# Transformer block stage on one core: splitting the normalized rows on token partitions and turning the fp16 halves with transposing DMA transfers

## What is computed

```python
h = _L0_tok_ref(x)                                   # attention over the 512 positions -> (64, 32, 512)
h = h + _L0_attn_ref(_layernorm(h, axis=-1), Wq, Wk, Wv, Wo, qn_w, kn_w)
h = h + _L0_ffn_ref(_layernorm(h, axis=-1), w1, w2, w3)
# _L0_attn_ref: 16 query heads and 4 key heads of 128; RMS norm and rotary embedding of q and k; causal; @ Wo.T
# _L0_ffn_ref:  sigmoid(x @ q(w1).T) * (x @ q(w2).T) @ q(w3).T with ternary q(w), hidden width 1408
```

## Time and profile before

| | |
|---|---|
| median of 3 executions | 1176.59 us (1174.29 to 1178.07) |
| the profiled execution | 1181.81 us |
| its span, first to last instruction | 1179.9 us |
| granted TensorE clock, mean over the span | 0.964 |
| busy: PE / DVE / ACT / POOL | 1097.3 / 722.2 / 422.4 / 433.5 us |

### The profile page before, as it was taken

The page is one execution under the profiler, slowest core; times in us unless marked ns, Lnnn a source line. Parts: engine busy times, 40 slices in busy tenths (PEclk is TensorE's granted clock), DMA queues, the critical chain, the costliest instruction groups (busy, mean ns, idle before and its releaser), DMA issues.

```text
span 1179.9 us, 22172 instructions
## 1 busy us (share of the span) xinstructions
PE 1097.3 (93%) x8768; PEld 609.3 (52%) x8768; DVE 722.2 (61%) x1293; ACT 422.4 (36%) x733; POOL 433.5 (37%) x334
## 2 busy tenths in 40 slices
PE   4999998889989569999999999999999999999987
PEld 2434333343334234664665756646646657566465
DVE  6687766766686255556655755665566557656642
ACT  1666545545555221322322412323223223223231
POOL 2001016664555254242351451433423614524320
PEclk9999898989998779999999999999999999999999
DMA  6988833554442100000000000000000000000000
GB/s 181 315 298 260 299 115 115 158 176 124 140 130 69 57 9 10 20 9 27 18 9 27 0 27 18 9 27 18 9 27 18 9 27 0 27 18 9 18 11 9
DMA packets 35767, 83.81 MB, mean 71 GB/s; under 512 B 4496, under 2 KB 5264, under 8 KB 35728
## 3 DMA queue, kind: packets, MB, share of 16 engines
q1 hardware_dynamic: 35728, 83.26, 22.8%
HBM read 49.43 MB, written 8.39 MB: 49 GB/s over the span
## 4 chain that ended last, share of the span: by engine, by line
PE 51%; DVE 8%; issue 4%; POOL 2%; ACT 0%; DMA 0%; SPq 0%; DVEq 0%; POOLq 0%
PE proj L973 7%; PE proj L974 7%; PE proj L975 7%; PE ffn_sum L1025 5%; PE ffn_sum L1026 5%; PE proj L1087 4%; PE proj L1088 4%; PE proj L1089 4%; PE transposed L967 3%; PE ffn_sum L1073 2%; PE transposed L1041 1%; PE proj L1059 1%; PE proj L1060 1%; DVE probs_t L930 1%; DVE scores L910 1%
## 5 line engine op out<-in xcount | busy, mean ns | idle before, releaser
L334 DVE TENSOR_REDUCE row_max<-score_rows 128x1 f32<-128x512 f32 x256 | 167.7, 686 | 94.0 <-PE score_rows L474 92.6
L700 POOL TENSOR_TENSOR roped<-rope_cos,rope_sin 128x512 f32<-128x512 f32 x80 | 101.7, 1271 | 328.3 <-DVE rope_sin L836 328.3
L293 ACT ACTIVATE exps<-score_cols 128x512 f32<-128x512 f32 x256 | 146.2, 600 | 140.4 <-PE score_cols L499 137.9
L1025 PE MATMUL ffn_sum<-x_hi,ffn_w 128*128 128x128 f16 x1408 | 167.0, 220 | 1.4 <-ACT x_hi L769 1.4
L1026 PE MATMUL ffn_sum<-x_lo,ffn_w 128*128 128x128 f16 x1408 | 166.8, 220 | 0.0
L735 ACT ACTIVATE squares<-proj 128x512 f32<-128x512 f32 x80 | 47.8, 597 | 323.4 <-PE proj L975 289.5
L973 PE MATMUL proj<-attn_slots,x_hi 128*128 128x512 f16 x384 | 147.8, 385 | 3.7 <-DVE rope_sin L836 2.2
L974 PE MATMUL proj<-attn_slots,x_hi 128*128 128x512 f16 x384 | 147.7, 385 | 0.0
L975 PE MATMUL proj<-attn_slots,x_lo 128*128 128x512 f16 x384 | 147.5, 384 | 0.0
L474 PE MATMUL score_rows<-k_parts,q_parts 96*128 96x512 f32 x256 | 127.4, 511 | 16.5 <-DMA k_parts<-qk_low 15.2
L1025 PEld LDWEIGHTS ffn_sum<-x_hi,ffn_w 128*128 128x128 f16 x1408 | 138.1, 98 | 6.4 <-DVE hidden L853 3.0
(11 more groups left out here) (108 smaller groups left out, 1724.7 us busy)
## 6 DMA issues: line engine op xcount, KB each, us to landing
raw_ffn<-in_w_ffn SPq DMA_DIRECT2D x24, 704.0 KB, 7.2
attn_slots<-in_w_attn SPq DMA_DIRECT2D x20, 512.0 KB, 10.8
qk_raw<-in_qk SPq DMA_DIRECT2D x16, 512.0 KB, 5.8
q_parts<-qk_high SPq DMA_DIRECT2D x32, 256.0 KB, 3.3
k_parts<-qk_high SPq DMA_DIRECT2D x32, 256.0 KB, 4.2
v_t<-in_v_t SPq DMA_DIRECT2D x16, 256.0 KB, 5.7
q_parts<-qk_low SPq DMA_DIRECT2D x16, 256.0 KB, 4.9
k_parts<-qk_low SPq DMA_DIRECT2D x16, 256.0 KB, 5.2
```

The lines of the kernel that those rows point to most:

```text
L293: nc.scalar.activation(E[:, (STEPS * g + u) % NE, :], ST[(STEPS * g + u) % 3][:, :], ACT.Exp, scale=TOK_SCALE).then_inc(exp_done, 1)
L334: nc.vector.reduce_max(row_max[:, g % 2, k:k + 1], S[n % NS][:, :], AX.X).then_inc(s_free, 1)
L1025: nc.tensor.matmul(dst, w, x2h[:, k * P:(k + 1) * P], start=(k == 0), stop=False)
```

## The change

Both places where normalized rows are turned are changed alike. The split into halves now happens on the rows as they lie, before they are turned: ScalarE rounds `xn` (or `x2n`) into `x_hi_rows` (or its twin), the low half is `xn` minus that. Then SyncE issues, for each half, one DMA transfer with `transpose=True` (128x512 fp16, SBUF to SBUF, 128 KB) into `x_hi` / `x_lo`, now laid out [P, KD, P]. TensorE's eight fp32 transposes per tile for `xn` and `x2n` are gone, and it waits for the two transfers instead. Along with it:

- the low half of the first norm moves from VectorE to GpSimd (`x_low`, behind `inv_std` and ahead of `rope_sum(n+1, 0)`); that of the second norm stays on VectorE and moves ahead by one chunk, between `rotate(n, 2)` and `rotate(n, 3)`;
- on ScalarE the rounding of `x2n` moves from behind `square(n, 3)` to behind `square(n, 1)`, the rounding of `xn` from behind `hidden_hi(n-1, 2)` to right behind the Exp;
- SyncE's loop over tiles is written out tile by tile; there `turn_x2(n-1)` and `turn_x(n+1)` stand between the loads of the rows and the store of the output.

```diff
-        xh, xl = sb("x_hi", [P, D], F16), sb("x_lo", [P, D], F16)
+        xhr, xlr = sb("x_hi_rows", [P, D], F16), sb("x_lo_rows", [P, D], F16)
+        xh, xl = sb("x_hi", [P, KD, P], F16), sb("x_lo", [P, KD, P], F16)
...
@@ block.sync
+            def turn_x(n):
+                sp.wait_ge(x_hi, n + 1)
+                sp.dma_start(xh[:, :, :], xhr[:, :], transpose=True).then_inc(x_turned, DMA)
+                sp.wait_ge(x_lo, n + 1)
+                sp.dma_start(xl[:, :, :], xlr[:, :], transpose=True).then_inc(x_turned, DMA)
...
                 if attn:
                     sp.wait_ge(h2_done, n)
                     sp.dma_start(h_res[:, :], h1[bass.ds(n * P, P), :]).then_inc(res_in, DMA)
                 if ffn:
+                    turn_x2(n - 1)
+                if more:
+                    turn_x(n + 1)
+                if ffn:
                     sp.wait_ge(o_out, n + START)
                     sp.dma_start(out[bass.ds((n - 1) * P, P), :], o_tile[:, :]).then_inc(out_done, DMA)
...
-            over_tiles(sp, body)
+            for n in range(NTT + 1):
+                body(n, n < NTT, n > 0)
@@ block.gpsimd
+            def x_low(n):
+                pool.wait_ge(x_hi, n + 1)
+                nc.gpsimd.tensor_tensor(xlr[:, :], xn[:, :], xhr[:, :], ALU.subtract).then_inc(x_lo, 1)
@@ block.scalar
             def take_x(n):
-                act.wait_ge(xt, n + 1)
-                nc.scalar.copy(xh[:, :], TR[0][:, :]).then_inc(x_hi, 1)
+                act.wait_ge(ln1, n + 1)
+                nc.scalar.copy(xhr[:, :], xn[:, :]).then_inc(x_hi, 1)
...
                 if attn:
-                    for c in range(1, KV):
+                    square(n, 1)
+                if ffn:
+                    act.wait_ge(ln2, n)
+                    nc.scalar.copy(x2hr[:, :], x2n[:, :]).then_inc(x2_hi, 1)
+                if attn:
+                    for c in range(2, KV + 1):
                         square(n, c)
-                if ffn:
-                    act.wait_ge(xt2, n)
-                    nc.scalar.copy(x2h[:, :], TR[1][:, :]).then_inc(x2_hi, 1)
-                if attn:
-                    square(n, KV)
@@ block.vector
-            def x_low(n):
-                dve.wait_ge(x_hi, n + 1)
-                nc.vector.tensor_tensor(xl[:, :], TR[0][:, :], xh[:, :], ALU.subtract).then_inc(x_lo, 1)
...
                 if attn:
-                    for c in range(2, KV):
+                    rotate(n, 2)
+                if ffn:
+                    dve.wait_ge(x2_hi, n)
+                    nc.vector.tensor_tensor(x2lr[:, :], x2n[:, :], x2hr[:, :], ALU.subtract).then_inc(x2_lo, 1)
+                if attn:
+                    for c in range(3, KV + 1):
                         rotate(n, c)
@@ block.tensor
                 if c == 0:
-                    pe.wait_ge(x_hi, n + 1)
-                    pe.wait_ge(x_lo, n + 1)
+                    pe.wait_ge(x_turned, 2 * DMA * (n + 1))
...
                 if f == 0 and m == 0:
-                    pe.wait_ge(x2_hi, n + 1)
-                    pe.wait_ge(x2_lo, n + 1)
+                    pe.wait_ge(x2_turned, 2 * DMA * (n + 1))
```

More of the change, by code:

```diff
@@ L676, in _, with turn_x2 @@
                 sp.dma_start(dst, src).then_inc(const_in, DMA)
+            def turn_x(n):
[3 more added lines that the diff above has]
+                sp.dma_start(xl[:, :, :], xlr[:, :], transpose=True).then_inc(x_turned, DMA)
+            def turn_x2(n):
+                sp.wait_ge(x2_hi, n + 1)
+                sp.dma_start(x2h[:, :, :], x2hr[:, :], transpose=True).then_inc(x2_turned, DMA)
+                sp.wait_ge(x2_lo, n + 1)
+                sp.dma_start(x2l[:, :, :], x2lr[:, :], transpose=True).then_inc(x2_turned, DMA)
+            turn_x(0)
             def body(n, attn, ffn):
-                if attn and not (isinstance(n, int) and n + 1 >= NTT):
+                more = attn and not (isinstance(n, int) and n + 1 >= NTT)
+                if more:
                     sp.wait_ge(ln1, n + 1)
@@ L783, in body @@
                             nc.scalar.activation(pr[:, :, :], sd[:, :, :], ACT.Exp).then_inc(exped, 1)
+                            if not last:
+                                take_x(n + 1)
                         if ffn and m == 1:
@@ L786, in body @@
                 if attn:
-                    if not last:
-                        take_x(n + 1)
                     act.wait_ge(pv, n + 1)
@@ L934, in body @@
                 if attn:
-                    if not last:
-                        x_low(n + 1)
                     for b in range(2):
@@ L1024, in gate_products @@
                         dst = FB[2 * (f % 2) + m][:, j * P:(j + 1) * P]
-                        nc.tensor.matmul(dst, w, x2h[:, k * P:(k + 1) * P], start=(k == 0), stop=False)
-                        ins = nc.tensor.matmul(dst, w, x2l[:, k * P:(k + 1) * P], start=False, stop=(k == KD - 1))
+                        nc.tensor.matmul(dst, w, x2h[:, k, :], start=(k == 0), stop=False)
+                        ins = nc.tensor.matmul(dst, w, x2l[:, k, :], start=False, stop=(k == KD - 1))
                 ins.then_inc(f1, 1)
@@ L1097, in body @@
                 if attn:
-                    for c in range(1, NPROJ - 2):
-                        project(n, c)
-                if ffn:
-                    transpose_x2(n - 1)
-                if attn:
-                    for c in range(NPROJ - 2, NPROJ):
+                    for c in range(1, NPROJ):
                         project(n, c)
@@ L1116, in body @@
                     down_products(n - 1, range(0, DOWN_FIRST))
-                if attn and not last:
-                    transpose_x(n + 1)
                 if attn:
```

28 lines of the change are left out of this document (9 added, 19 removed).

## The result

The changed kernel takes **1214.93 us** (median of 4 executions, 1213.87 to 1218.61), the kernel before 1177.33 on the same chip (4 executions, 1174.29 to 1178.99): a ratio of 1.032, 95% interval 1.029 to 1.036. It is slower by 37.6 us, where the forecast was 38.

A forecast was written before the change was run, and what follows sets the result against it. TensorE was taken to bound the kernel, busy 594 of 600 us. Second norm 27, first norm 7 and ends 4 us sum to 38 us over the median of 1176.59: 1214 us, range 1196 to 1255.

The forecast's parts named there:

- What leaves TensorE: Fp32 transposes leaving TensorE: those of xn worth nothing ahead of the probs_t wait, those of x2n at most 0.27 us.
- the third rival: No new wait decides: projection 4 starts 0.27 us earlier if square 2 ends in time; 1173 to 1179 us, chance 0.11.
- The second norm: x2n's rounding delays square 2 and the rotations, so projection 5 starts 1.8 us later per tile, 27 us in 15 tiles.
- The first norm: GpSimd's subtraction for xn makes VectorE's scaling of the probabilities wait 0.45 us per tile, 7 us in all.
- The transfers: Four transposing transfers per tile at 2.6 us each, hidden by 3.9 us (x2n) and 4.2 us (xn) before TensorE wants them.
- The ends: First tile's projection 0 starts 1.9 us later, last tile's gate products 2.0 us later; together 4 us.
- The sum: Whole kernel: 27 + 7 + 4 = 38 us more, on the median giving 1214 us.
- late transfers: Transposing transfers much slower than plain ones, showing per tile from 4 us on; 1254 us at 5.2 us each, chance 0.18.
- the granted clock: TensorE's new waits in each tile drop its clock to half for some 2 us, costing 30 us: 1244 us, chance 0.04.

The follow-up runs named there:

- the old places: Changed kernel with x2n's rounding back behind square 3 and its subtraction behind rotation 3, both norms still by transfers: 1201.68 us, ratio 1.0223 to the kernel before.
- The shorter chain: Changed kernel with square 2 before x2n's rounding and xn normalized earlier, plus VectorE's second-group hidden_lo moved behind the maximum's subtraction: 1179.98 us, 1.0023.

## Why the prediction was right

It was right in its sign, its size and, term by term, in the places.

- **What leaves TensorE** was put at 0.27 us per tile at most, though it is 0.88 us of work. The runs go further. In the one with the first norm alone the wait grew by all that the transposes of `xn` had taken, and against it the run with square 2 first shows that those of `x2n` were worth 0.12 us at projection 4, 0.27 less the 0.15 from the last reading of the bank to the matmul, and nothing at the gate products. So the 0.27 that the third rival counted on isn't there; the forecast itself didn't use it.
- **The second norm**, 1.8 us per tile: 1.88 measured, 1.24 of it at projection 4 (predicted 1.1) and 0.64 at projection 5 (predicted 0.7). The run with only this norm has a period 1.86 over before. That ScalarE's order is the cause, and not the transfer or VectorE, is shown by the run that moves square 2 alone: it leaves 0.42 of the 2.30. `mean_sq` at 0.74 us came as predicted.
- **The first norm**, 0.45 us per tile by the meeting of the scaling with GpSimd: 0.42, and shown by taking the subtraction away (0.43).
- **The transfers**, 2.6 us assumed from a plain one: 2.4 and 2.5, hidden in every tile but the first and last. The second one of `x2n` was issued at 710.19 and wanted when projection 5 ended, 2.6 us behind 711.57: 4.0 us later, where 3.9 was predicted. The run with the old places has it issued later, and there 0.8 us shows in each tile.
- **The ends**: 1.9 and 2.0 predicted, 1.9 and 2.3 measured. The 0.3 missing at the last tile is a step that the sum left out: the second transfer was issued at 1191.12, 0.5 us after its operand was there, as the queue was held by the first.
- **The sum**: (1.88 + 0.42) x 15 + 4.2 = 38.7 us; 37.6 measured between the medians, and 39.3 from `xn`'s end to the end of the span between the profiled executions. That the forecast of 38 lies within 0.4 us of the medians is closer than the measurement, whose interval is some 4 us to either side, and in so far luck.
- **The rivals**: late transfers did not show in this order, the granted clock stayed at 1.00 in the repeating tiles, and the third fell on the very point that it turned on, square 2's end at 706.72, 1.15 us behind `x2n` in place of ahead of it.

My theories of the later runs were less good. The shorter chain was one that only looked shorter, and the run without the subtraction lost its 0.43 us a tile but not the 7 us of the median that I expected. And the prediction saw the transfers only as a price, since it took TensorE's order as given: what they bring is that turned rows are ready without a place in TensorE's order, and that pays only once something is put into a wait.

## What to carry to other kernels

Where an engine works strictly in order, a step that is moved up waits there for its operand with all that is behind it; put it behind whatever is ready sooner, even on an engine that is idle two thirds of the time. Removing work from the bounding engine ahead of a wait only makes the wait longer, so count it as zero until something else fills the wait. And a transfer in place of a compute step needs its operand a latency earlier, so keep the old step where nothing covers that latency: the first and last tile here.

## What the runs showed of the hardware

- A transposing transfer of 128x512 fp16 (128 KB) within the chip's memory landed in 2.4 to 2.5 us, and held SyncE's queue for 1.19 to 1.27 us at its issue (1.32 once), where the plain store of 256 KB shows 0.34. Two in a row thus stand 1.24 us apart (1189.88 and 1191.12).
- 64 such transfers add 70584 - 35767 = 34817 packets, 544 each, nearly all under 512 bytes; the DMA share of the repeating tiles went from 0.05 to 0.10 with no transfer of the other queues slower by over 0.1 us where the change works (`h_ln` 2.7 to 2.8, `h_res` 2.6 and 2.6).
- VectorE's small `mean_sq`, 128x4, took 0.74 us beside an addition of GpSimd and 0.23 without it, three times its own length. The Trainium skill, SBUF — State Buffer, Who interferes with whom, counts `tensor_scalar` among the operations that can, under conditions on their operands, take the pair of ports shared with GpSimd; the row agrees, and the wait here was longer than the operation.
